# When the first product of weights and values may be placed among 200 unread transposes, in a fused attention and FFN layer on one core

## What is computed

```
scores = einsum('bhqd,bhkd->bhqk', q, k) * hd**-0.5
delta = pos[None, :] - pos[:, None]
mask = where(delta > 0, -log(delta + 1), 0);  -inf where delta < 0
out = einsum('bhqk,bhkd->bhqd', softmax(scores + mask), v) @ w_proj + b_proj
gate, y = fp4_linear(xn, w_gate), fp4_linear(xn, w_up)
x = x + out + fp4_linear(silu(gate) * y, w_down)
```

## Time and profile before

| | before |
|---|---|
| runs | 597.81, 599.75, 599.66 us |
| profiled execution, its time | 599.36 us |
| profiled execution, its span | 597.6 us |
| mean granted TensorE clock | 0.997 |
| PE, DVE, ACT, POOL busy | 562.5, 547.1, 409.3, 503.2 us |
| unread transposes (L1310) | 200 matmul rows |

### The profile page before, as it was taken

The page is one execution under the profiler, slowest core; times in us unless marked ns, Lnnn a source line. Parts: engine busy times, 40 slices in busy tenths (PEclk is TensorE's granted clock), DMA queues, the critical chain, the costliest instruction groups (busy, mean ns, idle before and its releaser), DMA issues.

```text
span 597.6 us, 11270 instructions
## 1 busy us (share of the span) xinstructions
PE 562.5 (94%) x3791; PEld 247.5 (41%) x3791; DVE 547.1 (92%) x1165; ACT 409.3 (68%) x868; POOL 503.2 (84%) x409
## 2 busy tenths in 40 slices
PE   5999999999899999999999999999999998999995
PEld 4677844544343434333333333342344343343322
DVE  5999989998999899999999999999998989999672
ACT  4668486675665567766776676767666767677793
POOL 7378888797998889798999989897988889798773
PEclk9999999999998999999999999999999999999999
DMA  7434344010000001000000000000000000000000
GB/s 203 103 104 113 110 99 108 2 74 8 1 3 1 2 1 60 39 1 2 1 1 1 20 1 2 1 2 2 1 2 19 2 0 2 2 0 2 2 2 18
DMA packets 14832, 16.66 MB, mean 28 GB/s; under 512 B 1639, under 2 KB 14216, under 8 KB 14360
## 3 DMA queue, kind: packets, MB, share of 16 engines
q1 hardware_dynamic: 14240, 15.70, 9.5%
q10 hardware_dynamic: 536, 0.26, 0.2%
HBM read 11.75 MB, written 4.01 MB: 26 GB/s over the span
## 4 chain that ended last, share of the span: by engine, by line
PE 53%; DVE 27%; issue 7%; ACT 7%; POOL 5%; POOLq 0%; ACTq 0%; DVEq 0%
PE psum L1467 14%; DVE mxp L1240 13%; PE psum L1425 13%; PE psum L1449 10%; DVE ring L1267 4%; PE psum L1310 3%; POOL ring L895 3%; PE psum L1381 2%; ACT ring L1049 2%; PE psum L1400 2%; PE psum L1428 2%; PE psum L1383 1%; PE psum L1452 1%; DVE psum L1222 1%; DVE xw L1218 1%
## 5 line engine op out<-in xcount | busy, mean ns | idle before, releaser
L895 POOL TENSOR_TENSOR ring<-ring,dist 128x1024 f32<-128x1024 f32 (+3 forms) x223 | 398.6, 1815 | 51.6 <-ACT ring L1049 50.8
L1240 DVE TENSOR_REDUCE mxp<-psum 128x1 f32<-128x512 f32 (+3 forms) x640 | 354.7, 598 | 16.6 <-PE psum L1425 13.9
L1049 ACT ACTIVATE ring<-psum 128x512 f32<-128x512 f32 (+3 forms) x446 | 221.8, 557 | 93.5 <-PE psum L1452 46.8
L1425 PE MATMUL psum<-kop,qop 96*128 96x512 bf16 (+3 forms) x640 | 198.4, 352 | 7.2 <-DVE mxp L1240 3.7
L1449 PE MATMUL psum<-qop,kop 128*128 128x512 bf16 (+3 forms) x640 | 191.2, 349 | 7.4 <-DVE mxp L1240 2.8
L1467 PE MATMUL psum<-ring,vaug 128*32 128x512 f32 (+3 forms) x1280 | 155.3, 556 | 2.5 <-POOL ring L895 1.9
L1267 DVE TENSOR_TENSOR ring<-psum,dist 128x512 f32<-128x512 f32 (+3 forms) x194 | 115.1, 620 | 12.0 <-ACT psum L1049 11.4
L1049 ACT ACTIVATE psum<-psum 128x512 f32<-128x512 f32 (+3 forms) x194 | 99.7, 545 | 31.7 <-PE psum L1449 19.0
L1425 PEld LDWEIGHTS psum<-kop,qop 96*128 96x128 bf16 x640 | 56.5, 97 | 134.6 <-DVE mxp L1240 45.5
L1449 PEld LDWEIGHTS psum<-qop,kop 128*128 128x128 bf16 x640 | 59.3, 97 | 83.6 <-DVE mxp L1240 19.7
L1428 PE MATMUL psum<-tri_q,identb 128*128 128x128 bf16 x256 | 55.9, 220 | 0.0
(11 more groups left out here) (134 smaller groups left out, 467.9 us busy)
## 6 DMA issues: line engine op xcount, KB each, us to landing
parts_dram<-qpart SPq DMA_DIRECT2D x18, 128.0 KB, 3.4
kop<-parts_dram SPq DMA_DIRECT2D x6, 384.0 KB
qop<-parts_dram SPq DMA_DIRECT2D x6, 384.0 KB
xin<-_attn_hidden_states_dram SPq DMA_DIRECT2D x4, 256.0 KB, 5.0
ring<-inv_dram SPq DMA_DIRECT2D x1, 1024.0 KB, 5.1
out_dram<-xin SPq DMA_DIRECT2D x4, 256.0 KB, 2.3
qop<-parts_dram SPq DMA_DIRECT2D x3, 288.0 KB
kop<-parts_dram SPq DMA_DIRECT2D x3, 288.0 KB
```

Source lines behind the costliest of these rows:

```text
L895: g_.tensor_tensor(slot(p)[:, 0:n], slot(p)[:, 0:n], both, ALU.mult).then_inc(weighed_pool, 1)
L1049: a_.activation(scores if pair_vec[p] else slot(p)[:, 0:n, e % 2], scores, ACT.Exp, scale=SCALE).then_inc(exp_done, 1)
L1240: v_.tensor_reduce(mxp[:, u % 2, 4 * a + j, c - g:c - g + 1], bank(*o)[:, 0:n], AX_X, ALU.max).then_inc(max_used, 1)
L1425: ins = mm(bank(*o)[:, 0:n], qop[0:K_MAX, u // NQ % 2, h, P * a:P * (a + 1)], kop[0:K_MAX, h, k0:k0 + n], start=True, stop=(c != g))
```

## The change

"pv" 0 loses its need for the last unread transpose. An unread transpose is no longer placed once "pv" 0 has been, and the loop ends although some of them are left in the queue. Nothing else of the source changes; the order of all items is worked out anew by plan().

```diff
@@ -212,8 +212,6 @@
         if s == first_step[u] and u:
             needs.append(("ACT", ("evac", u - 1)))
-        if s == 0 and FILL:
-            needs.append(("PE", ("warm", FILL - 1)))
         pe(("pv", s), 4 * P * blocks[s] + PV_SWITCH, needs, rank=5)
@@ -311,6 +309,8 @@
             free = len(free_banks(now))
+            if kind == "warm" and ("PE", ("pv", 0)) in seen:
+                return None
             if kind in ("pv", "hT", "down", "warm"):
                 return level
@@ -417,7 +417,7 @@
-        busy = [e for e in queues if any(left[e].get(k, 0) < len(q) for k, q in queues[e].items())]
+        busy = [e for e in queues if any(k != "warm" and left[e].get(k, 0) < len(q) for k, q in queues[e].items())]
```

## The result

Nine runs of the changed kernel have a median of 600.96 us (600.32 to 602.71), nine of the kernel before 599.66 us. The ratio is 1.0045, interval 1.003 to 1.0061: slower by 0.45%, 2.7 us. I had forecast 2.3 us faster.

A forecast was written before the change was run, and what follows sets the result against it. TensorE and VectorE, both near full, were taken to bound the kernel, with VectorE deciding. 1.7 us of VectorE's idle time plus 0.6 us from GpSimd gave 2.3 us off 599.66, so 597.4 us, range 592.6 to 602.8.

The forecast's parts named there:

- steps 1, 2: TensorE near 69 us: first product starts 5.6 us sooner; 29 unread transposes left out free 3.2 us, 171 stay.
- step 3: ScalarE's gap before 76.10 us: exps 16 to 21 move about 5.5 us ahead, the fourth chunk's fills with them.
- step 4: Worth of the change: 1.7 us of VectorE's idle time at 80 to 90 us, plus 0.6 us from GpSimd.
- one of my signs of being wrong: Forecast is wrong if VectorE's idle time over the whole span doesn't fall.
- The pair that I gave to GpSimd: One pair more for GpSimd between 70 and 80 us spares VectorE 1.27 us; half counted, 0.6 us.
- the split: Rival: four pairs of weighing go from GpSimd to VectorE, 5.1 us more work, 602.5 us; 0.20 including worse order.
- step 5: After the early start: the gain passes on to the end; reordering gives or takes 1 to 3 us, entered at 0.
- "faster" at 0.46: Chance given to a faster kernel, against 0.29 for the same time and 0.25 for slower.
- The clock: Rival: holes at 69 to 76 us drop TensorE's clock; 598.9 us with one fall, 600.4 with a second; chance 0.06.
- The range: Whole-kernel time from 592.6 us, the larger gain with 1.5 us of reordering, to 602.8 us.
- Absorbed: Rival: VectorE is full, holes only move and 1.7 us of idle returns elsewhere; 599.7 us, chance 0.14.

The follow-up runs named there:

- exchange of heads and tails: Four kernels joining either kernel's order up to the planner's 100 us with either's order after it; medians 599.48, 599.52, 602.29 and 601.30 us.
- new tail: The changed kernel's order after the planner's 100 us; behind the kernel before's order up to there 602.29 us, behind the changed kernel's own 601.30 us.
- new head: The changed kernel's order up to the planner's 100 us; followed by the kernel before's order 599.52 us, by the changed kernel's own 601.30 us.
- FILL = 205: Kernel before with 205 unread transposes in place of 200, the order planned anew: 605.36 us, ratio 1.0107.
- the four constants: Planner constants CHUNK_AT, FFN_AT/FFN_GAP, POOL_QUEUE and LAST_QUEUE moved: kernel before 595.34 us (ratio 0.9938), changed kernel 593.52 us (0.9908).
- the head with the old tail: Changed kernel's order up to the planner's 100 us, then the kernel before's order: 599.52 us, ratio 1.0011.
- four pairs: Early against late start: changed kernel against kernel before, new head against old with old tail and with new tail, and both kernels with the four constants.
- the second control: Changed kernel's order item for item, laid out by a planner following that order, another PSUM bank for 978 of 1394 items: 601.30 us, ratio 1.0029.

## Why the prediction was wrong

- **What bounds the kernel; where the product goes; how many are left out** (steps 1, 2): right. 69.05 us on the clock of the trace before, where I had about 69.0; 171 transposes are left.
- **ScalarE** (step 3): right in kind, too large. Exps resume 2.7 us sooner and the fills 4.3, not 5.5. The three DMA issues of unit 3's rows (72.78, 1.80 us) and a copy stand ahead of the exps in ScalarE's order; I had counted them as little work and not as a queue to be waited for.
- **What it is worth** (step 4): mis-sized. VectorE's idle time there fell, but by less. From 60 to 90 us it was 0 + 0 + 1.69 before; from 61.77 to 91.77 it is 0.93 in the changed kernel. That is 0.8 us and not 1.7. Over the whole span it rose, from 50.5 to 53.2 us (1.7 of it ahead of the first L1345 row), one of my signs of being wrong. The pair that I gave to GpSimd went to VectorE: 196 weighings and not 192. That stays under the 198 from which the split would have decided, so this rival is out.
- **What failed is step 5.** I wrote that a different order "can give or take 1 to 3 us" and entered it at 0. The exchange of heads and tails shows what it was for this change: the new tail costs 1.1 us behind the new head and 3.2 behind the old, against a head that is worth from a loss of 0.5 to a gain of 1.6 us and not 2.3. About 1 us more came with the allotment of the PSUM banks, for which I had no term. And the size that I allowed was too small in general: FILL = 205 moves the time by 5.9 us, and the four constants by 4.1 us in the kernel before. With a term that size beside a gain of 2.3 us, the sign was not to be had from the first 100 us, and "faster" at 0.46 claimed too much.
- **The clock**: I had put its fall at 69 to 76 us. It came at 595, in the idle waits of the last three products, and costs 0.9 us. The kernel before has the same idle waits, but in its profiled execution the last projection was over before the clock fell.
- **The range**: its upper end, 602.8, is the 602.5 of the rival with 0.3 us added, not the 1.5 that the text names. The measured time lies inside it either way.
- **Absorbed** was nearest for the head with the old tail (599.52 against 599.48), but for another reason: there 1.3 us were spared and went to a fall of the clock.

Open: which items of the new order, and which banks, cost the 1.7 us by unit 15 isn't settled; unit 9, where the weights pass falls back, isn't the place. And what the early start with its order is worth on the mean over orders I know from four pairs only: +2.7, +0.5, -1.6 and -1.8 us by the ratios. That it is a gain in general isn't shown.

## What to carry to other kernels

Where a list scheduler writes the order of a nearly full pipeline, every edit draws the whole order anew, and that draw can be larger than the edit's own worth. Measure the edit with the old order kept behind it, or over several draws, before you keep or drop it, and look for idle time at the join. Read a lead from an engine that is full, not from a milestone of one pass: 5.2 us at unit 0 were 0.7 us of VectorE's time. Then draw again on purpose: a better order gave 4.1 us here, the edit less than 2. And look at the last few microseconds by themselves: waits there can put TensorE on its slow clock for the last product, and a few unread transposes prevented it here.

## What I had not expected of the hardware

The first q and k products take one of two times, whatever the kernel. Here are the changed kernel's, and under them those of the kernel before:

```profile
10.56 3.75 PE L1329 MATMUL psum<-xnT,wa 128*128 128x512 f32 x4 [0.78 <-ACT xnT L950]
```

```profile
10.57 1.96 PE L1329 MATMUL psum<-xnT,wa 128*128 128x512 f32 x4 [0.78 <-ACT xnT L950]
```

3.75 to 1.96 is nearly the ratio of the two clocks, though the clock column says 1.00 in both traces at that time. That the clock is the cause isn't shown. It shifts all that follows by 1.8 us, which is nearly the distance of the two groups of runs.

Unread transposes do hold the clock. Where 29 of them were left out, the first product moved ahead and no other work took their place, it fell to 0.50 at 74 us behind a stretch in which TensorE had been busy 0.72 of 2 us; with 18 of them put in at the end, it no longer fell before the last projection. The same order with other PSUM banks (the second control) made its evacuation of unit 15 0.6 us earlier than the changed kernel's, and its runs about 1 us faster.
